# Causal attention and a gated FFN on one core: score passes on two float32r pieces of q and k in the two halves of the array's height, in place of three bfloat16 pieces over most of it

## The reference

```python
xn = layernorm(x)
qkv = einsum('btd,ed->bte', xn, w_in)            # 16 heads of 16 channels
att = q @ k^T / sqrt(16)                         # per head, 2048 x 2048
att = where(causal, att, 0.0)                    # masked scores are 0, not -inf
att = softmax(att); out = (att @ v) @ w_out^T
r = sigmoid(xr @ W_r^T); k2 = relu(xk @ W_k^T)**2; ffn = r * (k2 @ W_v^T)
y = x + out + ffn        # xr, xk: mixes of xn and xn one token earlier
```

## Time and profile before

| | |
|---|---|
| median of 3 runs | 1340.07 us |
| span of the profiled execution (first to last instruction) | 1332.9 us |
| the other 7.2 us of the median | around the span (the profiled execution's own device time is not given apart from its span) |
| PE busy | 1165.0 us (87%) |
| DVE busy | 949.8 us (71%) |
| ACT busy | 747.9 us (56%) |
| POOL busy | 364.2 us (27%) |
| mean granted TensorE clock | 0.950 |
| moved by DMA | 79.55 MB |

### The profile page before, as it was taken

One profiled execution on the slowest core, in us unless ns is written; L12 is line 12 of the kernel. 1 busy time (PEld: TensorE's weight loads), 2 busy tenths in 40 slices (PEclk: granted clock), 3 DMA queues, 4 the chain that ended last, 5 costly groups with the idle time before them and its releaser, 6 DMA issues.

```text
span 1332.9 us, 26802 instructions
## 1 busy us (share of the span) xinstructions
PE 1165.0 (87%) x7680; PEld 508.3 (38%) x7680; DVE 949.8 (71%) x1921; ACT 747.9 (56%) x1553; POOL 364.2 (27%) x716
## 2 busy tenths in 40 slices
PE   2999488889998799879896999699879996999998
PEld 1666355433343243324332333233323332333345
DVE  5777388878688668866785689568766885689822
ACT  1544233256765576557564766476547664766673
POOL 6121011333323132413132223222232233224221
PEclk9999699989999899989997999799889998999999
DMA  2446933371007100810063006300540054002023
GB/s 87 142 158 169 178 111 111 111 92 45 6 1 98 43 6 3 97 43 6 4 82 59 6 2 79 62 6 3 65 77 6 2 64 77 6 2 73 5 84 115
DMA packets 59124, 79.55 MB, mean 60 GB/s; under 512 B 6112, under 2 KB 48480, under 8 KB 57952
## 3 DMA queue, kind: packets, MB, share of 16 engines
q1 hardware_dynamic: 57824, 73.56, 27.8%
q0 software_dynamic: 1152, 4.19, 1.0%
HBM read 43.78 MB, written 29.36 MB: 55 GB/s over the span
## 4 chain that ended last, share of the span: by engine, by line
PE 56%; DMA 10%; DVE 7%; issue 3%; ACT 2%; SPq 1%; DVEq 1%; ACTq 0%; POOL 0%; POOLq 0%
PE ps_s L1046 16%; PE ps_o L1060 16%; PE ps_m L209 14%; DMA q_op<-shift_t 10%; DVE part_max L220 5%; PE ps_o L1070 2%; PE ps_m L1092 2%; PE ps_m L213 2%; ACT probs L928 2%; PE ps_x L1037 1%; PE ps_x L1038 1%; DVE row_max L233 1%; DVE turned L963 1%; SPq L775 1%; PE ps_x L1023 1%
## 5 line engine op out<-in xcount | busy, mean ns | idle before, releaser
L220 DVE TENSOR_REDUCE part_max<-ps_m 128x1 f32<-128x512 f32 (+3 forms) x1200 | 669.1, 603 | 249.0 <-PE ps_m L213 130.7
L928 ACT ACTIVATE probs<-ps_s 128x512 f32<-128x512 f32 (+3 forms) x1280 | 614.0, 535 | 365.2 <-PE ps_s L1046 359.9
L1046 PE MATMUL ps_s<-q_op,k_op 99*128 99x512 bf16 (+3 forms) x1280 | 444.1, 360 | 75.7 <-DMA q_op<-shift_t 62.7
L209 PE MATMUL ps_m<-k_op,q_op 96*128 96x512 bf16 (+3 forms) x1200 | 411.2, 359 | 23.5 <-DVE part_max L220 20.4
L1060 PE MATMUL ps_o<-probs,v_sb 128*32 128x512 f32 (+3 forms) x2560 | 304.1, 548 | 0.0
L876 POOL TENSOR_SCALAR_AFFINE_SELECT probs<-probs 128x128 f32<-128x128 f32 x512 | 146.3, 295 | 567.6 <-ACT probs L928 560.0
L1046 PEld LDWEIGHTS ps_s<-q_op,k_op 99*128 99x128 bf16 x1280 | 123.4, 99 | 388.2 <-ACT probs L928 225.3
L209 PEld LDWEIGHTS ps_m<-k_op,q_op 96*128 96x128 bf16 x1200 | 118.8, 99 | 145.3 <-DVE part_max L220 90.8
L843 POOL TENSOR_TENSOR diag_weight<-ident,masked_weight 128x2048 f32<-128x2048 f32 x32 | 115.5, 3610 | 122.1 <-ACT masked_weight L895 122.1
L213 PE MATMUL ps_m<-mask,ident 128*128 128x128 bf16 x470 | 103.4, 222 | 0.1
L1060 PEld LDWEIGHTS ps_o<-probs,v_sb 128*32 128x32 f32 x2560 | 51.0, 109 | 89.5 <-issue 47.0
(11 more groups left out here) (85 smaller groups left out, 831.6 us busy)
## 6 DMA issues: line engine op xcount, KB each, us to landing
parts_d<-parts SPq DMA_DIRECT2D x48, 256.0 KB, 3.0
q_op<-parts_d SPq DMA_DIRECT2D x48, 256.0 KB, 14.2
k_op<-parts_d SPq DMA_DIRECT2D x48, 256.0 KB, 15.8
vpad_d<-v_pad SPq DMA_DIRECT2D x32, 256.0 KB, 3.2
v_sb<-vpad_d SPq DMA_DIRECT2D x8, 1024.0 KB, 25.8
x_in<-x SPq DMA_DIRECT2D x8, 512.0 KB, 4.6
ffn_d<-ffn SPq DMA_DIRECT2D x8, 512.0 KB, 3.2
attn_t<-normed SPq DMA_DIRECT2D x128, 32.0 KB, 2.0
```

Source lines behind the costliest of these rows:

```text
L209: last = pe.matmul(ps_m[:, f % ring, 0:width], self.q_op[0:ROWS, p, h, q0:q0 + P], self.k_op[0:ROWS, p, h, pc * CH:pc * CH + width], start ...
L220: dve.tensor_reduce(self.part_max[:, u % 2, h * SUB + s, pc:pc + 1], ps_m[:, f % ring, 0:width], AX_X, ALU.max).then_inc(self.piece_reduce ...
L928: act.activation(probs[:, slot % PRING, 0:width], ps_s[:, slot % SRING, 0:width], ACT.Exp).then_inc(probs_ready, 1)
L1046: pe.matmul(ps_s[:, slot % SRING, 0:CH - q0], k_op[0:KROWS, p, h, kt * P:(kt + 1) * P], q_op[0:KROWS, p, h, u * CH + q0:(u + 1) * CH], sta ...
```

## The change

q and k are cut into two pieces instead of three, of the type float32r (a 4-byte type). Three products, (0,0), (1,0), (0,1), replace six, so 48 rows replace 96, and with two shift rows 50 replace 99. Two heads of a group lie in partitions 0 to 63 and the other two in 64 to 127 (`rows_of`), and `HEAD_AT` = (0, 2, 1, 3) makes neighbouring scores and neighbouring pieces (`piece`) use different halves. The widths of the products stay. The mask product on the diagonal is split in two (128 and 64 columns) that fit in 64 rows. Pieces now follow each pair of heads, and the values the fourth head. DRAM and SBUF hold q and k in 4-byte elements: the same bytes per load (32 rows of 8 KB a DMA, where there were 64 of 4 KB), a third more per store. ACT loses `middle_part`, DVE one of two steps per part, `max_step` two of six steps, and `place_shift` issues 4 DMAs instead of 3.

```diff
-Q_PARTS = (0, 1, 2, 0, 1, 0)
-K_PARTS = (0, 0, 0, 1, 1, 2)
+Q_PARTS = (0, 1, 0)
+K_PARTS = (0, 0, 1)
 ROWS = HD * len(Q_PARTS)
-KROWS = ROWS + 3
+SHIFT_PARTS = 2
+KROWS = ROWS + SHIFT_PARTS
+HALF = 64
+HEAD_AT = (0, 2, 1, 3)
...
-MAX_STEPS = 6
+MAX_STEPS = 4
...
-    hs, pc = divmod(f - PIECE0[u], u + 1)
-    h, s = divmod(hs, SUB)
-    return u, h, s, pc, (CH if pc < u else P * (s + 1))
+    pair, e = divmod(f - PIECE0[u], 2)
+    js, pc = divmod(pair, u + 1)
+    j, s = divmod(js, SUB)
+    return u, 2 * e + j, s, pc, (CH if pc < u else P * (s + 1))
+def rows_of(h, rows):
+    return slice(h // 2 * HALF, h // 2 * HALF + rows)
...
-        self.q_op = sb("q_op", [P, 2, GH, T], BF16)
-        self.k_op = sb("k_op", [P, 2, GH, T], BF16)
+        self.q_op = sb("q_op", [P, 2, GH // 2, T], F32R)
+        self.k_op = sb("k_op", [P, 2, GH // 2, T], F32R)
...
     def load_group(self, sp, i, p):
         for r in range(len(Q_PARTS)):
-            rows = slice(r * HD, (r + 1) * HD)
-            sp.dma_start(self.q_op[rows, p], self.parts_in[Q_PARTS[r], 0, i, p]).then_inc(self.q_loaded[p], 16)
-            sp.dma_start(self.k_op[rows, p], self.parts_in[K_PARTS[r], 1, i, p]).then_inc(self.k_loaded[p], 16)
+            for e in range(2):
+                rows = slice(e * HALF + r * HD, e * HALF + (r + 1) * HD)
+                sp.dma_start(self.q_op[rows, p].bitcast(F32),
+                             self.parts_in[Q_PARTS[r], 0, i, p, e]).then_inc(self.q_loaded[p], 16)
+                sp.dma_start(self.k_op[rows, p].bitcast(F32),
+                             self.parts_in[K_PARTS[r], 1, i, p, e]).then_inc(self.k_loaded[p], 16)
...
-        last = pe.matmul(ps_m[:, f % ring, 0:width], self.q_op[0:ROWS, p, h, q0:q0 + P],
-                         self.k_op[0:ROWS, p, h, pc * CH:pc * CH + width], start=True, stop=(pc < u))
+        rows, half = rows_of(h, ROWS), rows_of(h, HALF)
+        last = pe.matmul(ps_m[:, f % ring, 0:width], self.q_op[rows, p, h % 2, q0:q0 + P],
+                         self.k_op[rows, p, h % 2, pc * CH:pc * CH + width], start=True, stop=(pc < u))
         if pc == u:
-            last = pe.matmul(ps_m[:, f % ring, s * P:width], self.ident16[:], self.mask16[:], start=False, stop=True)
+            pe.matmul(ps_m[:, f % ring, s * P:width], self.pick16[half, 0], self.mask16[half, 0],
+                      start=False, stop=False)
+            last = pe.matmul(ps_m[:, f % ring, s * P + HALF:width], self.pick16[half, 1], self.mask16[half, 1, HALF:P],
+                             start=False, stop=True)
...
-            def rest_of(n, par, j):
             def low_part(n, par, j):
-                dve.wait_ge(mid_ready, n * 4 + j + 1)
-                dve.tensor_tensor(parts[:, par, 2, j], rest[:, j % 2], parts[:, par, 1, j],
-                                  ALU.subtract).then_inc(parts_ready, 1)
+                dve.wait_ge(hi_ready, n * 4 + j + 1)
+                dve.scalar_tensor_tensor(parts[:, par, 1, j], ps_qk[:, j % 2], SCALE if j < CC else 1.0,
+                                         parts[:, par, 0, j], ALU.mult, ALU.subtract).then_inc(parts_ready, 1)
...
-                for part in range(3):
-                    sp.dma_start(q_op[ROWS + part:ROWS + part + 1, p, :, u * CH:(u + 1) * CH],
-                                 shift_t[part * GH:(part + 1) * GH, u % 2]).then_inc(shift_loaded[u % 2], 16)
+                for part in range(SHIFT_PARTS):
+                    for e in range(2):
+                        row, at = e * HALF + ROWS + part, part * GH + e * 2
+                        sp.dma_start(q_op[row:row + 1, p, :, u * CH:(u + 1) * CH].bitcast(F32),
+                                     shift_t[at:at + 2, u % 2]).then_inc(shift_loaded[u % 2], 16)
...
-                        for h in range(GH):
-                            score_tile(p, u, kt, h, G)
-                            if not (nxt and last):
-                                for f in pieces_of(u, kt * GH + h):
-                                    ops.score_piece(pe, ps_m, MRING, f, 1 - p if nxt else p, (G + (nxt > 0)) * PIECES)
-                            if h == 2:
+                        for at in range(GH):
+                            score_tile(p, u, kt, at, G)
+                            if at % 2 == 1 and not (nxt and last):
+                                for hs in range(kt * GH + at - 1, kt * GH + at + 1):
+                                    for f in pieces_of(u, hs):
+                                        ops.score_piece(pe, ps_m, MRING, f, 1 - p if nxt else p, (G + (nxt > 0)) * PIECES)
+                            if at == GH - 1:
```

146 lines of the change are left out of this document (66 added, 80 removed).

## The result

The changed kernel is slower, by far: 1563.3 us, the median of six runs (1544.1 to 1583.7), against 1338.6 for the kernel before in the same session. The ratio is 1.1547, with a 95% interval of 1.1521 to 1.1574. The forecast was 1260. The six fall into a faster three (1544 to 1550) and a slower three (1577 to 1584), and the relatives of this kernel with float32r in halves scatter alike; medians here are over all executions, ratios over the faster ones only, and most profiled executions of such kernels, this one (1583.7) too, are of the slower.

The account below looks back on a forecast made before the run. A group was held to have a fixed part (load and shift, over units 0 and 1) and a PE-paced part (units 2 and 3). 1332.9 less 66.5 + 7 + 6 = 79.5, plus 7.2, gave 1260; range 1208 to 1345.

Parts of the forecast that it names:

- What a score costs: PE's score products: two array halves overlap fully and float32r keeps bfloat16's 0.22 us pace, so 0.11 us per paired score.
- The doubt that this part spent itself on: Score products on PE: whether halves overlap, and whether float32r runs at bfloat16's pace (0.22 us) or float32's (0.90).
- Units 2 and 3, "DVE is next": Units 2 and 3 of seven groups: DVE replaces PE as limit, gaining 9.5 us a group, 66.5 in all.
- the 5.5 us that it gave unit 3: Unit 3 with pieces: DVE at 0.92 full needs 50.3 us, against a window of 56.0; gain 5.5.
- DVE 0.99 full: Upper bound for units 2 and 3: DVE fuller than assumed gains 13 us a group, 91 in all.
- this is in the 0.92: Unit 3: bursts of pieces with values behind them may not feed DVE; its assumed fill of 0.92 covers that.
- Units 0 and 1 at nothing: Units 0 and 1: no net change; PE is faster but waits longer for the shift, under a 31.3 us load.
- Last group, 7 us gained: Last group, no pieces or load: score pairs less mode switches save 5 us in unit 3, 2 in unit 2.
- mode switches: Unit 3 of the last group: output tiles use the full array, one more tile-shape switch per key tile, 0.12 us.
- Token stage, 6 us: Token stage: DVE loses the third-piece step, 2.4 us over about three later chunks, gaining 6 (bounds 0 and 10).
- The rival "the clock": DVE-paced stretches: short PE gaps bring the clock to 1.2 GHz, costing 11 us a group, 1420 in all; chance 0.04.
- The rival "float32r at its full price": Scores and pieces: float32r costs as float32, 0.90 us per score pair, total near 1700; chance 0.03.

Follow-up runs that it names:

- e5: A kernel of its own: PE alone runs eleven product mixes, each but the first behind idling; 512-wide products in halves take 0.107 us (bfloat16) and 0.112 (float32r).
- e7: The changed kernel in bfloat16, next group's load issued behind unit 2's shift, pieces in the order of the kernel before: 1218.4 us, ratio 0.9099.
- e13: The changed kernel in bfloat16, load issued behind unit 2's shift, pieces still in pairs, values behind the third score: 1216.9 us, ratio 0.9096.
- e12: The changed kernel in bfloat16, load issued behind unit 2's shift, the change's order kept: 1286.8 us, ratio 0.9627.
- e1: The changed kernel with the next group's load issued behind unit 2's shift instead of ahead of it: 1462.6 us.
- e2: The kernel before with the next group's load issued behind unit 2's shift: 1278.2 us, ratio 0.9555.
- e8: The changed kernel (float32r) with late load and old order, every score on rows 0 to 113, adding two heads: 1375 us, ratio 1.0261.
- e15: The changed kernel in bfloat16 with the old order of pieces and values, load early as before: 1223.9 us, ratio 0.9138.
- e11: The changed kernel with bfloat16 in place of float32r and nothing else changed: 1290.9 us, ratio 0.9624.
- e6: The changed kernel (float32r in halves) with the load behind unit 2's shift and the old order: 1407 us, ratio 1.0341.
- e14: As e6, but scores of units 0 and 1 and pieces beside them use rows 0 to 113, adding two heads: 1339.1 us, ratio 1.0017.
- e9: A kernel of its own: sixteen product mixes behind idle stretches, nothing of the reference computed; four mixes stayed at 1.2 GHz to their end.
- e10: The kernel before with late load, q and k cut to two bfloat16 pieces, all in the lower half: 1614.9 us, clock 0.783.

## Why the prediction was wrong, point by point

Lengths of units are taken from the first closing product of one unit (`ps_o<-diag_weight`) to that of the next, the same in each kernel; the first unit of all starts at the first score.

- *What a score costs.* Right. Forecast 0.11 us a score in a pair: measured 0.107 in bfloat16 and 0.112 in float32r (e5), 0.12 in the changed kernel. The doubt that this part spent itself on was not where the loss lay.
- *Units 2 and 3, "DVE is next".* This step failed. It priced PE's products at 2.4 GHz and left the clock to a rival. In the changed kernel unit 2 of group 1 runs at a clock of 0.53 and takes 51.1 us, where before it took 31.9; unit 3 has 0.86 and takes 67.1, where before it took 52.5, with DVE busy 43.69 and PE 62.54. The size was off too. In e7, where the clock is 1.00 in both units and the order is the old one, the two units of group 1 gain 2.0 and 2.5 us, not 9.5 together; in e13, at a clock of 1.00 too, 0.7 and 1.4. DVE is 0.88 full in unit 3 of e7 (44.14 of 50.0) where 0.92 was taken, and PE is still busy 47.08, though the forecast had it under 0.8. Part of the 5.5 us that it gave unit 3 was never there: its window of 56.0 us was cut 3.5 wider than the unit. And at DVE 0.99 full its own terms give nearly 15 us a group, not 13; that bears on no conclusion.
- *"this is in the 0.92".* Also failed. I saw that the order had moved, named the bursts of pieces, and let a fill of 0.92 cover them. The bursts cost nothing in e13. What cost 70 us there (e12 to e13) was the values moved by one place, and it works through ACT and the scores' ring, which I had not looked at. The evidence was in the rows of the order that I had shown, and in ACT's mean of 0.535 us for an exponential of a score (L928 before) against a values pass of 1.00.
- *Units 0 and 1 at nothing.* Right on the load (32.9 us against 31.3) and on the sum: the two units take 49.0 to 50.0 us in groups 1 to 6, where they took 47.8 to 49.7. Wrong on the wait, which was to grow and fell from 62.7 to 42.4: PE was not faster there in each group, since in groups 2, 4 and 6 the clock fell while unit 1 still ran (at 624.2 in group 2). And the stall's cost is the idle time and the slow return behind it; the return was priced at 0.5 us, from a kernel with 99 rows. e1 shows 100 us for 42.4 of waiting.
- *Last group, 7 us gained.* It lost 24. Unit 2 took 45.4 us instead of 33.3, at a clock of 0.81. Unit 3 took 53.3 instead of 41.1, at the full clock. The place of the values is 8 of these 12 (50.4 in e12, 42.6 in e13 and e7), the type 3 (53.3 against 50.4). The last 1.5 fit the mode switches that I priced at 0.12 us per key tile. In e7 the output tile starts 0.32 us behind the score ahead of it, 0.09 more than before, and the next score 1.06 us behind the output tile, 0.19 more; that eats the 0.21 that the pair saves (the fourth score has no partner).
- *Token stage, 6 us.* The first score stands at 262.8 instead of 273.2: 10.4 gained, just outside the bounds of 0 to 10. Part of it is luck: 8.4 us are there already at the end of the first four chunks (DVE's `ffn` step at 109.9 instead of 118.3), for which the forecast had nothing. The last three chunks together are 4 us shorter, not 6. The first unit of attention then takes 28.5 us instead of 18.8, at a clock of 0.50, and the gain is gone. The pieces beside the chunks wait 19.6 us for the first load, as before (18.6). With half the bytes it is 5.1 us (e7), and the first score stands at 244.4: the bytes of that load were a term that I had not written.
- *The rival "the clock"* had 0.04 and 1420. It named the right resource and half of the condition. Short gaps do stand where the clock falls: in unit 2 of group 1 at 518.4, behind waits for ACT of 0.48 and 0.36 us. But what makes the loss large is that it then stays down where PE has hardly a gap (busy 99% of the next 20 us, and 35.57 of the 36 from 473). The row that I held against it, a clock of 1.00 in the tail of unit 2, was of a kernel with 99 rows in use, and could say nothing on 50.
- *The rival "float32r at its full price"* was wrong as to the stream. A part of it was true: the weight load has float32's price, 192 ns, and this is, as I read it, most of the 97 us with full rows (e2 to e8). I had the row for it, and used it only where nothing overlaps.

What the 225 us are, by the runs: the halves and two pieces in bfloat16 with the order kept gain 114 (before to e15); the order loses 67 (e15 to e11), by e13 through the place of the values; the type loses 272 (e11 to the change). The type's price in the late, old setting can be taken apart in the profiled executions, 196 us (e7 1221.8 to e6 1418.2). Of these, 19 lie ahead of attention (first score at 244.4 and 263.5). In units that both kernels ran at 0.92 or more, e6 needs 14.3, 24.2, 32.9 and 54.0 us, e7 13.8, 22.3, 29.9 and 50.0: 9.4 us a group, 75 in all. That leaves some 100 for the clock, and e14, 82 us shorter than e6 although its first score stands 13 us later (it clears rows first, as e8 does), gives most of them back. Such parts aren't strictly additive: the order costs 53 us with full rows and a clock of 0.95, and 130 where the clock is low.

Open: why the key tile in float32r halves gets its clock back within 8 us in e9, but stays low through all 36.7 us of unit 1 in five groups of e6. Narrow pieces with masks, which e9 shows to stay low, are a part of these units; that they decide it was not tried.

## What to carry to other kernels

Rows of the array that stand idle are not only unused: here the clock stayed low for long where products used half of them (e5, e9, e10), and came back when more were used (e14). Before packing small products, ask how much of the array works at once, and find the price with the type that will be used, at both clocks and at its narrowest width. And when a change reorders one engine's queue, follow every ring that the queue shares with another engine, by the number of its banks, and not only the one that the change is about.
